# First layer of a two-layer kernel: the first step begins with a quarter of the tokens and half of each weight

## The reference, cut to what matters

```
xn = layernorm(x)                       # (4, 512, 128), over 128 features
xq, xk, xv = xn @ wq, xn @ wk, xn @ wv  # 16 heads of 64
# 8 chunks of 64 tokens, one after the other, W and b carried (per sequence and head)
lr  = sigmoid(xk @ theta + theta_bias);  eta = clip(1/(1..64) + alpha, 0) * lr / 64
Z1  = xk @ W + b;  x_hat = (Z1 - mean) / std
grad_output = gamma * x_hat + beta - (xv - xk)
grad_x = gradient through the normalisation
W, b = W - (eta * xk).T @ grad_x,  b - sum(eta * grad_x)
Zq  = xq @ W + b;  out = xq + gamma * normalised(Zq) + beta;   result += out @ wo
# experts: softmax of xn @ Wg over the tokens, top 32 tokens of each of 16 experts
```

## Time and profile before

| | us |
|---|---|
| median of 3 runs | 975.94 (974.56 to 976.08) |
| the profiled execution | 973.86 |
| its span, first to last instruction | 971.7 |
| PE busy | 889.8 (92%) |
| DVE busy | 786.3 (81%) |
| POOL busy | 626.3 (64%) |
| ACT busy | 556.4 (57%) |

### The profile page before, as it was taken

The page is one execution under the profiler, slowest core; times in us unless marked ns, Lnnn a source line. Parts: engine busy times, 40 slices in busy tenths (PEclk is TensorE's granted clock), DMA queues, the critical chain, the costliest instruction groups (busy, mean ns, idle before and its releaser), DMA issues.

```text
span 971.7 us, 19701 instructions
## 1 busy us (share of the span) xinstructions
PE 889.8 (92%) x7768; PEld 618.2 (64%) x7768; DVE 786.3 (81%) x1182; ACT 556.4 (57%) x828; POOL 626.3 (64%) x571
## 2 busy tenths in 40 slices
PE   1788999999998897799999999999999999999997
PEld 1566778778786677556666656655656666666554
DVE  7768988899886626797888897898788788888876
ACT  3444566666654362456657556666665765656653
POOL 4357888888784002868559559657757855955862
PEclk9888999999999899799999999999999999999999
DMA  8100000000000302101101111101201210220110
GB/s 228 25 2 1 2 3 2 3 2 2 3 3 1 88 2 87 39 38 64 56 12 60 65 27 62 63 4 61 73 25 55 64 47 24 70 75 20 45 52 21
DMA packets 24963, 38.26 MB, mean 39 GB/s; under 512 B 9316, under 2 KB 15480, under 8 KB 22824
## 3 DMA queue, kind: packets, MB, share of 16 engines
q1 hardware_dynamic: 23240, 34.74, 11.7%
q10 hardware_dynamic: 1632, 2.27, 0.7%
HBM read 28.29 MB, written 1.43 MB: 31 GB/s over the span
## 4 chain that ended last, share of the span: by engine, by line
PE 54%; POOL 18%; DVE 13%; issue 8%; ACT 5%; DMA 1%; SPq 0%; POOLq 0%; ACTq 0%; DVEq 0%
PE bank L1135 9%; POOL hdl L1108 8%; PE bank L1137 8%; PE bank L1136 8%; PE bank L1399 5%; POOL hdh L1106 4%; PE bank L1291 3%; PE quad L1187 2%; DVE hdh L954 2%; PE quad L1440 2%; POOL arena L1061 2%; POOL arena L1055 2%; PE quad L1178 2%; PE bank L1250 2%; PE quad L1335 2%
## 5 line engine op out<-in xcount | busy, mean ns | idle before, releaser
L947 DVE TENSOR_REDUCE mx<-quad 128x4 f32<-128x2048 f32 x64 | 146.4, 2287 | 41.3 <-PE quad L1430 41.2
L1106 POOL CAST hdh<-xn 128x512 fp32r<-128x512 f32 x96 | 65.6, 683 | 144.9 <-ACT xn L616 144.9
L631 ACT ACTIVATE ex<-quad 128x2048 f32<-128x2048 f32 x64 | 120.6, 1884 | 51.7 <-PE quad L1440 51.6
L1108 POOL TENSOR_TENSOR hdl<-hd,hdh 128x512 fp32r<-128x512 f32 x96 | 129.5, 1349 | 7.7
L1108 POOL TENSOR_TENSOR hdl<-xn,hdh 128x512 fp32r<-128x512 f32 x96 | 128.4, 1338 | 7.7
L616 ACT ACTIVATE hd<-bank,b1c 128x512 f32<-128x512 f32 x128 | 88.0, 687 | 64.4 <-POOL hdl L1108 30.3
L1135 PE MATMUL bank<-hdh,W2h 128*128 128x512 f32 x256 | 110.9, 433 | 3.0 <-DVE hdl L957 1.5
L616 ACT ACTIVATE xn<-bank,b1c 128x512 f32<-128x512 f32 x128 | 87.9, 687 | 33.9 <-PE bank L1137 16.5
L1137 PE MATMUL bank<-hdl,W2h 128*128 128x512 f32 x256 | 100.5, 393 | 0.0
L1136 PE MATMUL bank<-hdh,W2l 128*128 128x512 f32 x256 | 100.3, 392 | 0.0
L1135 PE MATMUL bank<-cH,W1h 128*128 128x512 f32 x192 | 81.2, 423 | 0.7 <-DVE cL L974 0.7
(11 more groups left out here) (301 smaller groups left out, 2200.4 us busy)
## 6 DMA issues: line engine op xcount, KB each, us to landing
cwB<-gate_rows SPq DMA_DIRECT2D x16, 1024.0 KB, 4.7
kx<-kqh SPq DMA_DIRECT2D x32, 64.0 KB, 2.1
qx<-kqh SPq DMA_DIRECT2D x32, 64.0 KB, 2.1
ex<-in_L_ffn_W SPq DMA_DIRECT2D x1, 1024.0 KB, 5.9
kx<-kql SPq DMA_DIRECT2D x16, 64.0 KB, 2.1
qx<-kql SPq DMA_DIRECT2D x16, 64.0 KB, 2.1
rec<-rec_rows SPq DMA_DIRECT2D x32, 32.0 KB, 2.1
out<-fin SPq DMA_DIRECT2D x4, 256.0 KB, 2.3
```

The lines of the kernel that those rows point to most:

```text
L631: act.activation(ex[:, t % 2, :, :], quad[:, :, :], ACT.Exp, scale=float(AD) ** -0.5).then_inc(ROUND["exps_ready"], 1)
L947: dve.tensor_reduce(mx[:, t, :], quad[:, :, :], AX_X, ALU.max, negate=True).then_inc(ROUND["score_max"], 1)
L1106: pool.tensor_copy(hdh[:, m % RING, :], tile(n)).then_inc(ROUND["pool_split"], 1)
L1108: pool.tensor_tensor(hdl[:, m % RING, :], tile(n), hdh[:, m % RING, :], ALU.subtract).then_inc(ROUND["pool_split"], 1)
```

## The change

Tokens are cut into quarters: quarter k is the tile k of each of the four sequences (128 tokens of each). `HALF` cuts a weight's 1024 columns in two. Quarter 0 is loaded first, by SP's queue; the other three come by ACT's queue behind wv and gamma. Ahead of the loop only quarter 0 is normalised, turned and split, only the first half of wk, wu, gg and of the target's row is made, and two of the four key tiles. POOL does nothing ahead of `wu_low`, except memsets and two small copies. W1 is centred once on DVE, and ACT copies the result to the other three sequences.

The rest stands in the steps: quarter 1 is centred and normalised by ACT in step 0 and turned and split in step 1, quarter 2 in steps 2 and 3, quarter 3 in steps 3 and 4. The second halves of theta and wu are POOL's in step 0, the queries' weights POOL's in steps 1 and 2, wog in step 3 instead of 2. Keys are computed from step 0 on. The rates come in two parts, for two chunks in step 1 and for six in step 5 (`token_rates`); so does the sigmoid. The router's weights are made in step 3, its logits and `choice(0)` in step 5, just ahead of the folded output weights; `choice(1)` to `choice(6)` stand in steps 7, 10, 13, 16, 19, 22, the exponential in step 9, the turning of the ranks in step 30. The rows of the choice have a tile of their own, `choice_rows`, instead of parts of attnT.

The core of the diff, by engine in the order SP, ACT, DVE, POOL, PE:

```diff
-            for b in range(2):
-                sp.dma_start(x[:, b * NT:(b + 1) * NT, :], xd[:, b]).then_inc(x_loaded[0], 16)
+            sp.dma_start(of_part(x[:, :, :], 0), xd[:, :, 0]).then_inc(x_loaded[0], 16)
...
+            sp.wait_ge(zeros_ready, 2)
...
-            for b in range(2, B):
-                act.dma_start(x[:, b * NT:(b + 1) * NT, :], xd[:, b]).then_inc(x_loaded[1], 16)
-            act.dma_start(th[:, :], A["L0_attn_theta"].rearrange("h d a -> a (h d)").broadcast_to([P, D])).then_inc(theta_loaded, 16)
             act.dma_start(wv[:, :], A["L0_attn_wv"]).then_inc(wv_loaded, 16)
             act.dma_start(gamB[:, :], A["L0_attn_gamma"].rearrange("h a d -> a (h d)").broadcast_to([P, D])).then_inc(gamma_loaded, 16)
+            for b in range(B):
+                act.dma_start(x[:, b * NT + 1:(b + 1) * NT, :], xd[:, b, 1:]).then_inc(x_loaded[1], 16)
+            act.dma_start(th[:, :], A["L0_attn_theta"].rearrange("h d a -> a (h d)").broadcast_to([P, D])).then_inc(theta_loaded, 16)
 
...
+            def deviations(k):
+                act.wait_ge(norm_sums, k + 1)
+                act.activation(stat(2, k), stat(1, k), ACT.Sqrt, bias=C("ln_eps"), scale=1.0 / P).then_inc(dev_ready, 1)
+
+            def centred(k):
                 act.wait_ge(norm_step, k + 1)
-                act.activation(xsq[:, 8 * k:8 * k + 8, :], xn[:, 8 * k:8 * k + 8, :], ACT.Square).then_inc(squares_ready, 1)
...
+                act.activation(stat(3, k), stat(0, k), ACT.Copy, scale=-1.0 / P).then_inc(squares_ready, 1)
+                act.wait_ge(squares_ready, 3 * k - 1)
+                for b in range(B):
+                    n = b * NT + k
+                    last = act.activation(xn[:, n, :], x[:, n, :], ACT.Identity, bias=st[:, 3, n:n + 1])
+                last.then_inc(squares_ready, 1)
+                act.wait_ge(squares_ready, 3 * k)
+                act.activation(xsq, of_part(xn[:, :, :], k), ACT.Square).then_inc(squares_ready, 1)
+
+            def normalised(k):
+                act.wait_ge(norm_rdev, k)
+                for b in range(B):
+                    n = b * NT + k
+                    last = act.activation(xn[:, n, :], xn[:, n, :], ACT.Identity, scale=st[:, 1, n:n + 1])
+                last.then_inc(norm_done, 1)
...
+            target_weights(0), target_row(0)
...
+                if s < 4:
+                    squares(s), take_xk(s), deviation(s), take_u(s)
+                    if s == 0:
+                        for b in (2, 3):
+                            act.activation(Wst[:, b, :, :], Wst[:, 0, :, :], ACT.Copy).then_inc(weights_centred, 1)
+                        centred(1), take_keys(s), deviations(1), normalised(1)
+                    if s == 1:
+                        sigmoid(0), tokens_high(1), take_keys(s), tokens_whole(1), target_weights(1), target_row(1)
+                        act.wait_ge(wq_loaded, 16)
+                        act.activation(wqh[:, :], wq[:, :], ACT.Copy).then_inc(wq_high, 1)
+                    if s == 2:
+                        act.wait_ge(wq_turned, 1)
+                        for n in range(2):
+                            act.activation(wqT[:, 4 * n:4 * n + 4, :], (bank[0], misc)[n][:, :].rearrange("p (a c) -> p a c", a=4), ACT.Copy).then_inc(wq_turned_taken, 1)
+                        centred(2), take_queries(s), take_keys(s), deviations(2), normalised(2)
+                    if s == 3:
+                        bias_high(0), centred(3)
+                        act.wait_ge(wq_low, 2)
+                        take_queries(s), tokens_high(2), take_keys(s), deviations(3), normalised(3), tokens_whole(2)
+                    continue
                 take_xk(s), take_turned(s - 2), squares(s), squares_q(s), take_u(s)
                 if s % 2:
                     bias_high((s - 3) // 2)
-                deviation(s), take_queries(s), deviation_q(s), take_att(s - 2), take_keys(s)
...
+                deviation(s), take_queries(s), deviation_q(s), take_att(s - 2)
+                if s == 4:
+                    tokens_high(3)
+                take_keys(s)
+                if s == 4:
+                    tokens_whole(3)
+                if s == 5:
+                    sigmoid(1)
                     act.wait_ge(out_weights, 1)
                     act.activation(Wqo[:, :], misc[:, 0:P], ACT.Copy).then_inc(out_weights_taken, 1)
                     act.activation(bo0[:, :], misc[:, P:P + 1], ACT.Copy).then_inc(out_weights_taken, 1)
-                if s == 4:
+                if s == 9:
+                    act.wait_ge(choice_step, 2)
+                    act.activation(rkp[:, 1, :], lgt[:, :], ACT.Exp, bias=es[:, 0:1], accum_out=es[:, 1:2]).then_inc(choice_exp, 1)
...
+            link(norm_sum(0))
+            link(dve.tensor_scalar(stat(3, 0), stat(0, 0), 1.0 / P, None, ALU.mult))
+            spread = lambda j: stat(j, 0).unsqueeze(2).broadcast_to([P, B, P])
+            dve.tensor_tensor(of_part(xn[:, :, :], 0), of_part(x[:, :, :], 0), spread(3), ALU.subtract).then_inc(norm_step, 1)
             dve.wait_ge(w0_loaded, 32)
             link(dve.tensor_reduce(m0[:, 0, 0:NP], W1s[:, :, :], AX_X, ALU.add))
-            dve.tensor_scalar(m0[:, 1, 0:NP], m0[:, 0, 0:NP], 1.0 / HD, None, ALU.mult).then_inc(w_mean_ready, 1)
-            for b in range(B):
...
+            link(dve.tensor_scalar(m0[:, 1, 0:NP], m0[:, 0, 0:NP], 1.0 / HD, None, ALU.mult))
+            norm_squares(0)
+            dve.wait_ge(dev_ready, 1)
+            link(dve.reciprocal(stat(1, 0), stat(2, 0)))
+            dve.wait_ge(squares_ready, 1)
+            dve.tensor_tensor(of_part(xn[:, :, :], 0), of_part(xn[:, :, :], 0), spread(1), ALU.mult).then_inc(norm_done, 1)
+            dve.wait_ge(wk_high, 1)
+            dve.tensor_tensor(wkl[:, HALF[0]], wk[:, HALF[0]], wkh[:, HALF[0]], ALU.subtract).then_inc(wk_low, 1)
+            dve.tensor_tensor(Wst[:, 0, :, :], W1s[:, :, :], m0[:, 1, 0:NP].unsqueeze(2).broadcast_to([P, NP, HD]), ALU.subtract).then_inc(weights_centred, 1)
+            tokens_low(0)
...
+                if s == 1:
+                    rates_biased_(0), tokens_low(1)
                 if s % 2:
                     bias_low((s - 3) // 2)
-                normed(s), rate_of(s - 1), gradient(s), update(s - 2), sum_gx(s), sum_gx_xhat(s)
+                normed(s)
+                if s == 1:
+                    rates_scaled(0)
+                if s == 3:
+                    tokens_low(2)
+                if s == 4:
+                    tokens_low(3)
+                if s == 5:
+                    rates_biased_(1), choice(0)
+                if s == 6:
+                    rates_scaled(1)
+                rate_of(s - 1), gradient(s), update(s - 2), sum_gx(s)
                 if s == 0:
-                    choice(0), choice(1)
-                elif s == 1:
-                    choice(2), choice(3)
-                elif s == 2:
-                    choice(4), choice(5)
-                elif s == 3:
-                    choice(6)
+                    theta(), token_rates()
+                sum_gx_xhat(s)
+                if s == 0:
+                    norm_squares(1), norm_reciprocal(1)
+                if s == 1:
+                    target_product(1), target_row(1), target_split(1)
+                if s in (2, 3):
+                    norm_squares(s), norm_reciprocal(s)
+                if s == 3:
+                    router_weights()
+                if s in (7, 10, 13, 16, 19, 22):
+                    choice((s - 4) // 3)
...
+            pool.wait_ge(wu_low, 1)
+            pool.wait_ge(wk_high, 2)
+            pool.tensor_tensor(wkl[:, HALF[1]], wk[:, HALF[1]], wkh[:, HALF[1]], ALU.subtract).then_inc(wk_low, 1)
...
+            def theta(k):
+                pool.wait_ge(theta_loaded, 16)
+                pool.tensor_tensor(th[:, HALF[k]], th[:, HALF[k]], wk[:, HALF[k]], ALU.mult).then_inc(theta_scaled, 1)
+
+            def target_weights():
+                pool.tensor_tensor(wu[:, HALF[1]], wk[:, HALF[1]], wv[:, HALF[1]], ALU.subtract).then_inc(wu_ready, 1)
+                pool.wait_ge(wu_ready, 2)
+                pool.tensor_tensor(wu[:, HALF[1]], wu[:, HALF[1]], gamB[:, HALF[1]], ALU.mult).then_inc(wu_ready, 1)
...
+            theta(0)
...
             for s in range(4 * NC + 1):
-                scaled(s), gx_xhat(s), rated(s - 1), part(s), less(s)
                 if s == 2:
+                    query_weights(1)
+                scaled(s)
+                if s == 0:
+                    theta(1)
+                gx_xhat(s), rated(s - 1), part(s)
+                if s == 0:
+                    target_weights()
+                less(s)
+                if s == 1:
+                    query_weights(0)
+                if s == 3:
                     pool.wait_ge(wo_loaded, 16 * 5)
...
+            turn_tokens(0)
             pe.wait_ge(wk_low, 1)
...
+            pe.wait_ge(CHUNK["tokens_low"], 1)
+            for m in range(2):
```

(35 more changed lines are left out.)

322 lines of the change are left out of this document (165 added, 157 removed).

## The result

The changed kernel takes 980.37 us, the median of 6 runs (977.33 to 986.23), beside 975.80 for the kernel before on the same chip (974.42 to 976.45). The ratio is 1.0057, with a 95% interval of 1.0032 to 1.0082: slower by 4.6 us, half a per cent. The profiled execution took 980.18 with a span of 978.4, against 971.7 before, so 6.7 in the profile. I had forecast slower, 985: the direction came, and about half of the size (4.6 for 9).

What follows compares the result with a forecast made beforehand. Bound: an in-order DVE/POOL/ACT round of 6.8 per step, or PE's attention products at 8.15. Start 23.4 earlier, spent by step 6 (2.1 later), plus 7.8 and 0.6: 10.5 later, forecast 985; 8-in-10 range 968 to 996.

Steps and rivals of the forecast that it cites:

- The start: Stretch before step 0's normalisation: W1's sum begins at 12.0, then pieces of 14.8; 23.4 us earlier than before.
- x(0): Start of DVE's normalisation multiplication (line 759 before the change) in step 0; forecast at 26.8 against 50.18.
- row by row: In the start's loads: the two DMA queues take turns one row against one, so W1 lands nearer its old time.
- Steps 0 to 4: First five loop steps: the quarters' pieces lengthen DVE's round of 6.8; sum 59.6 against 46.3.
- The first rival: Steps 0 to 4 swallow the pieces and stay at 46.3; kernel at 967 to 971; chance 0.22.
- Step 5: Rates, logits and output weights on PE, two round trips ahead of DVE's gradient: 19.4 instead of 7.2.
- the upper bound: For step 5: 16 more if all its pieces run at the low clock level.
- Steps 6 to 30: Steady loop: six moved choice steps cost 7.8, the exponential's table loads in step 9 cost 0.6.
- what would prove it wrong: Gaps behind the choice steps close again within the next steps; or step 5 starts before 76.
- The turned ranks: Turning of the ranks in step 30 costs 0, bounded above by 0.7 for eight transposes.
- x(31): Start of DVE's normalisation multiplication in step 31; forecast 10.5 later than before, with nothing different from there on.
- The second rival: Choice-step pauses drop the loop's clock to 0.85; six steps lose 1.3 each, 8 more, 993; chance 0.12.

Runs made afterwards that it cites:

- e1: Changed kernel without the replacements after each maximum, maxima 2 to 4, the comparison and the scan: 977.27 us, 1.0015 of the kernel before.
- e10: Changed kernel plus one more router-form matmul behind the logits in step 5, into rows nobody reads: 982.81 us, 1.0065 of the kernel before.
- e11: e9 with the router's weights and biases on DVE ahead of the third quarter's low part in step 3, not at the step's end: 969.37 us.
- e12: e11 with the quarters' sums of squares and reciprocals earlier on DVE in steps 2 and 3: 966.33 us, 0.9908 of the kernel before.
- e3: e2 with DVE taking the router's logits only behind the sum of step 5's gradient: 979.33 us, 1.0040 of the kernel before.
- e9: e7 with the last choice step behind step 20 instead of 17: 969.13 us, 0.9926 of the kernel before.
- e7: Changed kernel with the moves of e2, e5 and e6 together, and W1 loaded ahead of wk: 971.45 us, 0.9961 of the kernel before.
- e2: Changed kernel with the folded output weights made in steps 2 and 3 instead of step 5: 978.58 us, 1.0034 of the kernel before.
- e5: Changed kernel with choice steps behind 8, 9, 12, 13, 16, 17 and the exponential in step 12: 978.41 us, 1.0030 of the kernel before.
- e6: Changed kernel with theta's second half on POOL behind step 0's gradient-xhat product, its sum later on DVE: 979.85 us, 1.0062 of the kernel before.

## Why the prediction was right, point by point

**In short.** The mechanism was right: a shorter start, spent again in the early steps and in step 5, and a loop that loses by the moved choice steps. The size was about half: 4.6 by the medians for 9. Of the terms, the start came out to 0.1, steps 0 to 4 were put too high by 4.3, the loop by 1.1, and step 5 too low by 1.3, which is partly luck, since its error has the other sign and hangs on the clock's level.

**The start** was right. W1's sum began at 12.22 for 12.0 forecast, x(0) was at 26.75 for 26.8, and the pieces between them summed to 14.5 for 14.8 (bias rows to the square, for one, 22.48 to 24.83, 2.35 for 2.35). The 12.0 was a choice between bounds. My estimate by the Trainium skill (DMA: Bandwidth & Descriptors, Queues, rings and completion order) was 10 for the sum, and it did not come. The equal numbers of rows, 723 and 726, fit turns of one row and also turns of several rows that are alike in number, so neither nor these rows show how many make a turn; "row by row" was more than the rows said.

**Steps 0 to 4** took 55.27, not 59.6. By step, forecast and measured: 11.1 and 11.03, 13.3 and 11.47, 10.7 and 11.09, 14.4 and 12.46, 10.1 and 9.22. The terms that were mis-sized are in steps 1, 3 and, by 0.9, 4. I had built each step as DVE's round plus every piece on DVE. In step 1 the wait for the quarter's high part was 1.52 and not 2.65; PE turned the tokens at 2.4 GHz there, in 0.60. In e1 they came at 1.2 GHz (1.05), the wait was 2.61 and the step took 12.57, in e10 and e11 12.54 and 12.55. So that term was right for the lower level, and my 13.3 was 0.7 too long there and 1.8 in the changed kernel's profile. In step 3 the low part waited 2.31 and with its own 0.6 took 2.9, not 4.0, and the router's weights cost 0 for the 2.0 that I gave them; e11 and e12 showed that DVE's round does not set that step, but the chain over the quarter's reciprocal and ACT's four scalings, which I had as 0.4 in step 0, 0.7 in step 2 and nowhere in step 3. The first rival (these steps swallow the pieces, 46.3) did not come.

**Step 5** took 20.67, not 19.4. The terms of the sum: rates 1.58 (2.5 forecast), logits 3.62 (4.0), output weights 3.7 to 3.9 (3.8), the handoffs 0.55, 0.93 and 0.52. The rates were put 0.9 too high; the table's reload, 0.6 net in the sum, stood with its whole 1.28 (at 100.83) ahead of the root, for which DVE waited 2.31. What the sum lacked is the lower clock behind the pieces, 2.4 by e1, which I had only as the upper bound; at a clock of 1.00 the same step took 18.30, 1.1 under the forecast. The place of the chain was wrong, as e3 showed: PE's order, not DVE's gradient. I had expected DVE idle for 5 to 6 behind the logits; it waited 3.80 for them, and 5.69 later, behind its gradient.

**Steps 6 to 30** lost 7.3 and not 8.4 (198.72 - 191.42). Against the usual gaps: step 7 1.4, step 9 1.5 for the exponential, step 10 1.0, step 13 0.5, step 16 0.1, step 19 2.8, step 22 1.5, together 8.8. The 1.5 between are two steps behind a pause that took 7.55 instead of 8.30: PE had caught up. The prediction named such a regain as what would prove it wrong (if only x(6) then counted), and it occurred in part: 1.5 of 8.8 in the changed kernel, the whole of one slot in e9's step 20. Single sizes were off both ways: the exponential 1.5 for 0.6, since both table loads and the copies behind them came ahead of a root that DVE waits for; the scan 1.95 for 1.22; the slots in steps 13 and 16 together 0.6 for 0.9. By the Trainium skill (ScalarE: Activation LUTs, What ACT_TABLE_LOAD costs) a switch takes 2.66 with its drain; the rows again show 1.28, with the activation at 130.48, 0.01 behind the load's end, so the measured 1.28 holds here.

**The turned ranks** in step 30 cost nothing, as put: the gap is 7.41, and steps 14 and 26 of the same kernel, which have no such piece, take 7.40 and 7.41.

**The sum.** Forecast 10.5 at x(31) and at the end, measured 6.3 at x(31), 6.7 in the span and 4.6 in the medians. The 4.2 between the first two are 4.3 in steps 0 to 4, 1.1 in the loop, and 1.3 the other way in step 5. The 2 between profile and medians come from the kernel before: its profiled execution, 973.86, lies 1.9 under its median, the changed kernel's 0.2. Why is not shown.

**The second rival**, the clock in the loop, did not come in the changed kernel's profile (clock 1.00 from 102.69 to 301.41), but it did in e7's step 18 (2.0 by e9) and in e2's and e3's steps 23 and 24 (1.5 each). I had priced it at 1.3 a step. It may make the changed kernel's scatter (9 us between its runs, 2 to 4 for the kernel before): its two longest runs, 983.77 and 986.23, have the lowest mean clocks, 0.968 and 0.962, where the other four have 0.974 to 0.977. Where in the kernel the clock was lost in them is not shown, since only one execution was profiled.

## What to carry to other kernels

A fixed start is worth shortening only if the work taken out of it lands where an engine truly waits: here 23.4 us were won and 13.4 spent again in one step in which three small products, each with a handoff, stood in one row on TensorE. Put such pieces apart, one to a step, and put them into a wait and not at a step's end; before costing a piece at its length, follow the wait that ends the step, since in step 3 a piece of 1.4 cost nothing while moving a sum of 0.7 and a reciprocal won 2.4. In this loop, where two engines are nearly full, a pause of one engine was made up in the next step when it stood alone in a pair of steps bound by the other (e9's step 20), and two in a row cost 2.6 (e5's steps 16 and 17). And before an edit is judged by one profile, look at which level of the clock the execution met: in e6 a move worth 1.3 looked worthless for that reason.

## What the runs showed of the hardware that I had not expected

- The level of TensorE's clock at a given step differs between executions whose code is the same up to there. Step 1 took 11.47 when the transposes of wq and of the tokens ran at 2.4 GHz (changed kernel, x(1) at 37.78) and 12.57 when they ran at 1.2 (e1, x(1) at 37.75). Step 5 took 20.67 and 18.30 in the same two, this time the changed kernel at the lower level. What decides it wasn't found. The transposes of wq in step 1 of the changed kernel, then of e1:

```profile
39.29 0.60 PE L1444 MATMUL quad<-cst,arena 128*128 128x128 f32 x4
```
```profile
40.31 1.06 PE L1443 MATMUL quad<-cst,arena 128*128 128x128 f32 x4
```

- In e10, two matmuls of 64 output columns each, into different rows of one PSUM bank, ran side by side (88.29 and 88.35, 0.59 each). The filler's records even begin, at 87.87, before the last matmuls that stand ahead of it in the program.
- The scan took 1.95 in the changed kernel and in e5 where it was 1.22 before; it now reads its ones from a broadcast column and its data from another tile. Whether that or POOL beside it is the cause wasn't tried: POOL's `part` (line 1182) ran beside its first 0.87 in both, and nothing of POOL's beside the scan of the kernel before.
